# A graph layer in split single precision: one stationary operand for the edge sums, the bias moved to ScalarE

## What is computed

```python
h = jnp.maximum(_layernorm(x, axis=-1), 0.0)
agg = jax.ops.segment_sum(edge_features, tgt, num_segments=N_NODES)
counts = jax.ops.segment_sum(jnp.ones(...), tgt, num_segments=N_NODES)
agg = agg / jnp.maximum(counts, 1.0)[:, None]
combined = jnp.concatenate([agg, h], axis=1)
out = x + jax.nn.relu(combined @ W1 + b1) @ W2 + b2
```

## Time and profile before

| | |
|---|---|
| runs, median of 3 | 1381.35 us (1381.05 to 1381.44) |
| the profiled execution, its own time | 1381.12 us |
| its span, first to last instruction | 1379.1 us |
| mean granted TensorE clock | 0.989 of full speed |
| busy: PE / PEld | 1340.5 us / 1122.1 us |
| busy: DVE / ACT / POOL | 1202.3 us / 696.5 us / 533.0 us |

### The profile page before, as it was taken

One profiled execution on the slowest core, in us unless ns is written; L12 is line 12 of the kernel. 1 busy time (PEld: TensorE's weight loads), 2 busy tenths in 40 slices (PEclk: granted clock), 3 DMA queues, 4 the chain that ended last, 5 costly groups with the idle time before them and its releaser, 6 DMA issues.

```text
span 1379.1 us, 29845 instructions
## 1 busy us (share of the span) xinstructions
PE 1340.5 (97%) x7078; PEld 1122.1 (81%) x7078; DVE 1202.3 (87%) x2979; ACT 696.5 (51%) x1280; POOL 533.0 (39%) x709
## 2 busy tenths in 40 slices
PE   2799999999999999999999999999999999999998
PEld 0588888888888888888888888888888888888887
DVE  7598989898888989898988888898889898898986
ACT  3354545455554545454555545454545555454543
POOL 4334343433333343434333343434343443434341
PEclk7899999999999999999999999999999999999999
DMA  5567676766767676867667676758676766767672
GB/s 108 89 122 136 115 143 110 138 113 135 116 132 129 119 138 113 143 111 138 114 135 115 133 131 117 133 118 142 109 141 113 136 117 131 120 129 132 118 128 56
DMA packets 424904, 169.49 MB, mean 123 GB/s; under 512 B 323190, under 2 KB 424506, under 8 KB 424892
## 3 DMA queue, kind: packets, MB, share of 16 engines
q1 hardware_dynamic: 421608, 167.40, 67.0%
q10 hardware_dynamic: 3284, 1.97, 0.8%
HBM read 66.50 MB, written 51.40 MB: 85 GB/s over the span
## 4 chain that ended last, share of the span: by engine, by line
PE 96%; DVE 2%; DMA 1%; SPq 1%; issue 0%
PE P L815 26%; PE P L817 14%; PE P L795 13%; PE P L797 13%; PE P L796 13%; PE P L804 7%; PE P L805 7%; PE PA L785 2%; PE PA L784 2%; DVE below L597 1%; DMA X<-in_x_dram 0%; DMA dst_a<-in_dst_dram 0%; SPq L275 0%; DMA table_dram<-table 0%; SPq L276 0%
## 5 line engine op out<-in xcount | busy, mean ns | idle before, releaser
L815 PE MATMUL P<-w_both,H_hi 128*128 128x512 f32 x1568 | 552.1, 393 | 4.7 <-DVE H_lo L646 4.7
L530 ACT ACTIVATE H_hi<-P 128x512 fp32r<-128x512 f32 x392 | 234.6, 599 | 509.9 <-PE P L805 509.9
L817 PE MATMUL P<-w_both,H_lo 128*128 128x256 f32 x1568 | 442.5, 282 | 0.0
L646 DVE SCALAR_TENSOR_TENSOR H_lo<-P,H_hi 128x512 fp32r<-128x512 f32 x392 | 268.8, 686 | 108.4 <-ACT H_hi L530 101.8
L815 PEld LDWEIGHTS P<-w_both,H_hi 128*128 128x128 f32 x1568 | 295.3, 188 | 71.0 <-DVE H_lo L646 6.2
L795 PE MATMUL P<-HT_hi,w_hi 128*128 128x512 f32 x784 | 316.0, 403 | 19.5 <-DVE HT_lo L638 19.5
L797 PE MATMUL P<-HT_hi,w_lo 128*128 128x512 f32 x784 | 310.8, 396 | 0.0
L796 PE MATMUL P<-HT_lo,w_hi 128*128 128x512 f32 x784 | 310.4, 396 | 0.0
L817 PEld LDWEIGHTS P<-w_both,H_lo 128*128 128x128 f32 x1568 | 297.0, 189 | 4.5
L409 POOL TENSOR_TENSOR XB<-X,b_row 128x1024 f32<-128x1024 f32 x98 | 234.9, 2397 | 137.9 <-DVE O L657 137.9
L403 POOL TENSOR_TENSOR E_lo<-ES,E_hi 128x256 fp32r<-128x256 f32 x98 | 73.1, 746 | 416.0 <-ACT E_hi L510 416.0
(11 more groups left out here) (72 smaller groups left out, 1136.9 us busy)
## 6 DMA issues: line engine op xcount, KB each, us to landing
X<-in_x_dram SPq DMA_DIRECT2D x98, 512.0 KB, 4.2
HQ<-HN SPq DMA_DIRECT2D x388, 128.0 KB, 4.2
out_dram<-O SPq DMA_DIRECT2D x97, 512.0 KB, 4.8
ER<-in_edge_attr_dram SPq DMA_DIRECT2D x392, 32.0 KB, 1.8
DT<-table_dram SPq DMA_DIRECT2D x392, 1.0 KB, 1.7
w_raw<-in_L_gnn_W_dram ACTq DMA_DIRECT2D x4, 128.0 KB, 7.2
w_raw<-in_L_gnn_W_dram ACTq DMA_DIRECT2D x2, 256.0 KB, 8.6
HQ<-HN ACTq DMA_DIRECT2D x4, 128.0 KB, 4.1
```

Of the source, the lines that this page charges most:

```text
L530: act.activation(H1_hi[:, m, :], bank(m)[:], ACT.Relu).then_inc(s_1hi, 1)
L646: dve.scalar_tensor_tensor(out=H1_lo[:, m, :], in0=bank(m)[:], scalar=0.0, in1=H1_hi[:, m, :], op0=ALU.max, op1=ALU.subtract).then_inc(s_1 ...
L815: pe.matmul(out_bank(j)[:], H1_hi[:, m, rows], w2_both[:, m, :, :].rearrange("p a d -> p (a d)"), start=(m == 0), stop=False)
L817: last = pe.matmul(out_bank(j)[:, 0:D], H1_lo[:, m, rows], w2_both[:, m, 0, :], start=False, stop=(m == CH - 1))
```

## The change

It has three parts.

- E_hi and E_lo become two halves of one tile, E_both, so that a group's edges form one stationary operand of 128 columns. `edge_means` issues 4 products instead of 8; PA now has 128 rows, the sums of the high parts in rows 0 to 63 and those of the low parts in rows 64 to 127.
- QA is now the rounding of all 128 rows of PA, against W1's edge rows twice (wa_hi). QB holds the rounded sums in rows 0 to 63, against the low part of those weights, and in rows 64 to 127, in place of the ones, what rounding the high sums left over, against the high part.
- b1 is no longer a row of wb_lo. It is loaded as a column (b1_col), and ACT adds it as it applies the relu. ACT now reads each PSUM bank twice: once for H_hi, once for H1, the same relu in full precision; DVE subtracts the two from SBUF.

```diff
-            pool.memset(b1_raw[:], 0.0).then_inc(s_zero, 1)
...
-            pool.memset(QB[DE:P, :].bitcast(F32), 1.0).then_inc(s_const, 1)
...
-                pool.tensor_tensor(E_lo[b][:], ES[b][:], E_hi[b][:], ALU.subtract).then_inc(s_elo, 1)
+                pool.tensor_tensor(E_both[b][:, :, 1, :], ES[b][:], E_both[b][:, :, 0, :], ALU.subtract).then_inc(s_elo, 1)
...
-            for p in (64, 96):
-                act.dma_start(b1_raw[p:p + 1, :], b1.rearrange("(o h) -> o h", o=1)).then_inc(s_w[2], 16)
+            act.dma_start(b1_col[:], b1.rearrange("(m p) -> p m", p=P),
+                          allow_slow_non_contiguous=True).then_inc(s_w[2], 16)
...
-                act.activation(QB[0:DE, :], PA[0:DE, :], ACT.Copy).then_inc(s_qhi, 1)
+                act.activation(QA[:], PA[:], ACT.Copy).then_inc(s_qhi, 1)
                 act.wait_ge(s_qhi, 2 * t + 1)
-                act.activation(QA[0:DE, :], QB[0:DE, :], ACT.Copy).then_inc(s_qhi, 1)
+                act.activation(QB[0:DE, :], QA[0:DE, :], ACT.Copy).then_inc(s_qhi, 1)
...
-                    act.activation(H1_hi[:, m, :], bank(m)[:], ACT.Relu).then_inc(s_1hi, 1)
+                    act.activation(H1_hi[:, m, :], bank(m)[:], ACT.Relu, bias=b1_col[:, m:m + 1]).then_inc(s_1hi, 1)
+                    act.activation(H1[:, m, :], bank(m)[:], ACT.Relu, bias=b1_col[:, m:m + 1]).then_inc(s_1, 1)
...
-            act.activation(b1_hi[DE:P, :], b1_raw[DE:P, :], ACT.Copy).then_inc(s_whi, 1)
-            act.activation(wb_lo[64:96, :], b1_raw[64:96, :], ACT.Copy).then_inc(s_whi, 1)
+            act.activation(wb_lo[DE:P, :], wa_raw[DE:P, :], ACT.Copy).then_inc(s_whi, 1)
...
-                dve.tensor_tensor(QA[DE:P, :], PA[0:DE, :], QB[0:DE, :], ALU.subtract).then_inc(s_qlo, 1)
+                dve.tensor_tensor(QB[DE:P, :], PA[0:DE, :], QA[0:DE, :], ALU.subtract).then_inc(s_qlo, 1)
...
-                dve.scalar_tensor_tensor(out=H1_lo[:, m, :], in0=bank(m)[:], scalar=0.0, in1=H1_hi[:, m, :],
-                                         op0=ALU.max, op1=ALU.subtract).then_inc(s_1lo, 1)
+                dve.wait_ge(s_1, CH * t + m + 1)
+                dve.tensor_tensor(H1_lo[:, m, :], H1[:, m, :], H1_hi[:, m, :], ALU.subtract).then_inc(s_1lo, 1)
...
-            dve.tensor_tensor(wb_lo[96:P, :], b1_raw[96:P, :], b1_hi[96:P, :], ALU.subtract).then_inc(s_wblo, 1)
...
-                    pe.matmul(PA[0:DE, cols], E_hi[b][:, k, :], OH[b][:, k, :], start=(k == 0), stop=False)
-                    last = pe.matmul(PA[0:DE, cols], E_lo[b][:, k, :], OH[b][:, k, :], start=False, stop=(k == SUB - 1))
+                    last = pe.matmul(PA[:, cols], E_both[b][:, k, :, :].rearrange("p a d -> p (a d)"), OH[b][:, k, :],
+                                     start=(k == 0), stop=(k == SUB - 1))
```

More of the change, by code:

```diff
@@ L89, in build @@
         wa_raw = sb("wa_raw", [P, H])
-        b1_raw = sb("b1_raw", [P, H])
+        b1_col = sb("b1_col", [P, CH])
         w2_raw = sb("w2_raw", [P, CH, D])
@@ L95, in build @@
         wb_lo = sb("wb_lo", [P, H], F32R)
-        b1_hi = sb("b1_hi", [P, H], F32R)
         w2_both = sb("w2_both", [P, CH, 2, D], F32R)
@@ L138, in build @@
         ES = [sb(f"ES{b}", [P, SUB, DE]) for b in range(2)]
-        E_hi = [sb(f"E_hi{b}", [P, SUB, DE], F32R) for b in range(2)]
-        E_lo = [sb(f"E_lo{b}", [P, SUB, DE], F32R) for b in range(2)]
+        E_both = [sb(f"E_both{b}", [P, SUB, 2, DE], F32R) for b in range(2)]
         OH = [sb(f"OH{b}", [P, SUB, P], F32R) for b in range(2)]
@@ L146, in build @@
         QB = sb("QB", [P, TILE], F32R)
+        H1 = sb("H1", [P, CH, TILE])
         H1_hi = sb("H1_hi", [P, CH, TILE], F32R)
@@ L226, in build @@
         s_1hi = sem("s_1hi")
+        s_1 = sem("s_1")
         s_1lo = sem("s_1lo")
@@ L353, in _ @@
             pool.memset(dst_b[:], 1 << 20).then_inc(s_zero, 1)
-            pool.memset(b1_raw[:], 0.0).then_inc(s_zero, 1)
             pool.iota(thresholds[:], pattern=[[P, KS], [TILE, TILES]], base=0, channel_multiplier=0,
                       allow_small_or_imprecise_dtypes=True).then_inc(s_zero, 1)
-            pool.wait_ge(s_zero, 3)
+            pool.wait_ge(s_zero, 2)
             pool.iota(thresholds[:, :, TILES - 1:TILES], pattern=[[P, KS], [0, 1]], base=LAST, channel_multiplier=0,
@@ L375, in _ @@
             pool.wait_ge(s_const, 10)
-            pool.memset(QB[DE:P, :].bitcast(F32), 1.0).then_inc(s_const, 1)
+            pool.memset(ident[:], 0.0).then_inc(s_const, 1)
             pool.wait_ge(s_const, 11)
-            pool.memset(ident[:], 0.0).then_inc(s_const, 1)
-            pool.wait_ge(s_const, 12)
             pool.affine_select(out=ident[:], in_=ident[:], compare_op=ALU.not_equal, fill=1.0, base=0,
@@ L415, in _ @@
             pool.tensor_tensor(w1_lo[:], w1_raw[:], w1_hi[:], ALU.subtract).then_inc(s_wlo, 1)
-            pool.wait_ge(s_whi, 5)
+            pool.wait_ge(s_whi, 4)
             pool.tensor_tensor(w2_both[:, :, 1, :], w2_raw[:], w2_both[:, :, 0, :], ALU.subtract).then_inc(s_wlo, 1)
@@ L491, in _ @@
                 act.dma_start(wa_raw[a * DE:(a + 1) * DE, :], w1[0:DE, :]).then_inc(s_w[1], 16)
-            act.wait_ge(s_zero, 3)
-            for p in (64, 96):
-                act.dma_start(b1_raw[p:p + 1, :], b1.rearrange("(o h) -> o h", o=1)).then_inc(s_w[2], 16)
+            act.dma_start(b1_col[:], b1.rearrange("(m p) -> p m", p=P),
+                          allow_slow_non_contiguous=True).then_inc(s_w[2], 16)
             for a in range(2):
@@ L509, in edges_high @@
                 past(act, s_sum, t - 1)
-                act.activation(E_hi[b][:], ES[b][:], ACT.Copy).then_inc(s_ehi, 1)
+                act.activation(E_both[b][:, :, 0, :], ES[b][:], ACT.Copy).then_inc(s_ehi, 1)
             def transposed_high(t):
@@ L535, in _ @@
             act.activation(wa_hi[:], wa_raw[:], ACT.Copy).then_inc(s_whi, 1)
-            act.wait_ge(s_w[2], 32)
-            act.activation(b1_hi[DE:P, :], b1_raw[DE:P, :], ACT.Copy).then_inc(s_whi, 1)
-            act.activation(wb_lo[64:96, :], b1_raw[64:96, :], ACT.Copy).then_inc(s_whi, 1)
+            act.activation(wb_lo[DE:P, :], wa_raw[DE:P, :], ACT.Copy).then_inc(s_whi, 1)
+            act.wait_ge(s_w[2], 16)
             act.wait_ge(s_w[3], 32)
@@ L749, in _ @@
             onehot(0, 0)
-            dve.wait_ge(s_whi, 3)
+            dve.wait_ge(s_whi, 2)
             dve.tensor_tensor(wb_lo[0:DE, :], wa_raw[0:DE, :], wa_hi[0:DE, :], ALU.subtract).then_inc(s_wblo, 1)
-            dve.tensor_tensor(wb_lo[96:P, :], b1_raw[96:P, :], b1_hi[96:P, :], ALU.subtract).then_inc(s_wblo, 1)
             means_low(0)
@@ L774, in _ @@
             pe.matmul(PA[0:1, 0:1], ones_f[0:EP, :], fall[:], start=True, stop=True).then_inc(s_found, 1)
-            pe.wait_ge(s_const, 13)
+            pe.wait_ge(s_const, 12)
             def edge_means(t, b):
@@ L846, in _ @@
             pe.wait_ge(s_wlo, 2)
-            pe.wait_ge(s_wblo, 2)
-            pe.wait_ge(s_whi, 5)
+            pe.wait_ge(s_wblo, 1)
+            pe.wait_ge(s_whi, 4)
             step(0, 0)
```

## The result

| | before | changed |
|---|---|---|
| median of the runs | 1381.39 us (1381.05 to 1384.72) | 1448.19 us (1447.89 to 1448.84) |
| ratio | | 1.0482, 95% interval 1.0467 to 1.0496 |
| the profiled execution, its own time | 1381.12 us | 1447.89 us |
| its span; mean granted TensorE clock | 1379.1 us; 0.989 | 1446.3 us; 0.989 |

What follows compares the result with a forecast made beforehand. PE was taken to bound the kernel, at 13.54 us a tile. Stop less edge gain, 96 x (0.23 - 0.09) = 13.4 us, on 1381.1 gave 1394.5 us, 1.0% slower; range 1376 to 1412, the forecast's own 1388 to 1401.

Steps and rivals of the forecast that it cites:

- H_lo itself keeps its length: DVE's hidden-layer subtraction: 686 ns before with one operand in PSUM, 687 ns for L638 wholly from SBUF, so no lengthening.
- PE's stop: Ahead of the first product with block 3, PE waits for a late H_lo: 0.23 us a tile, bounds 0.05 and 0.41.
- the start of block 2's H_lo: On DVE, H_lo of block 2 also waits for the second activation and starts 0.64 us later, at 719.00.
- the edge sums: Edge stage on PE, four products on 128 columns instead of eight: PE gains 0.53 - 0.44 = 0.09 us a tile.
- the bias operand: ACT's two activations read the bias from a tile: 0.09 us more on the interval and on the length.
- the means: Second products of the means cost PE nothing; DVE's part arrives just in time, with 0.06 us remaining.
- b1's load: At the start, b1 fetched in 512 four-byte pieces: 6.8 us, covered by ACT's 9.89 us wait for POOL.
- The signs: Wrong if the PE-from-H_lo line has few entries, the waits show the means instead, or the tile is under 13.54 us.
- the line that the forecast named: "PE P <- DVE H_lo" in the waits of PE, with some 96 entries and about 20 us.
- The fifth: Rival: the means come late too, for instance through each H_lo's second wait; 0.10 us there gives 1404 us; chance 0.09.
- The first: Rival: all 0.18 us falls on ACT's bias operand, stop 0.41, tile loses 0.32, 1412 us; chance 0.12.
- The second: Rival: second activation fits into DVE's slack at block 2's H_lo (0.41 us); 1377 or 1372.5 us; chance 0.09.

Runs made afterwards that it cites:

- last version: Changed kernel with one biased activation, H_lo as max(sum, -b1) - H_hi from PSUM, missing b1 put back through b2: 1373.67 us, ratio 0.9943.
- the third experiment: Changed kernel without DVE's wait for the first activation (s_1hi), H_lo still with both operands in SBUF: 1407.09 us, ratio 1.0184.

## Why the prediction was wrong, point by point

The 66.8 us, put together from the medians of the runs (those of the kernel before differ by up to 0.2 us):

| step | from, to | us |
|---|---|---|
| merged edge sums, one activation with bias, low part from PSUM | before 1381.2, last version 1373.7 | -7.5 |
| second activation, plain, and two waits; no bias operand | 1373.7, 1389.45 | +15.8 |
| bias operand on both activations | 1389.45, 1406.4 | +16.9 |
| both operands of H_lo in SBUF | 1406.4, 1448.2 | +41.8 |

The last step has no price of its own: it is 41.8 us with both waits, 6.6 with one, and 23 in the kernel before, as the start of H_lo falls against XB's.

- **The step that failed: "H_lo itself keeps its length: 686 ns before with one operand in PSUM, and 687 ns for L638".** The rows are right and the inference isn't. The prediction put the lengthening at nothing; H_lo took 1066 ns in the mean, 1719 beside an XB and 679 elsewhere, and with both waits in place that is 41.8 of the 66.8 us. L638 is the same operation, but not beside the same neighbour, as the timeline of the kernel before shows:

```profile
701.10 0.69 DVE L646 SCALAR_TENSOR_TENSOR H_lo<-P,H_hi 128x512 fp32r<-128x512 f32 x1
701.20 2.40 POOL L409 TENSOR_TENSOR XB<-X,b_row 128x1024 f32<-128x1024 f32 x1 [1.44 <-DVE O L657]
...
702.44 0.69 DVE L646 SCALAR_TENSOR_TENSOR H_lo<-P,H_hi 128x512 fp32r<-128x512 f32 x1
...
707.78 0.62 POOL L398 TENSOR_TENSOR ES<-ER,DT 128x256 f32<-128x256 f32 x1
708.29 0.67 DVE L638 TENSOR_TENSOR HT_lo<-HT,HT_hi 128x512 fp32r<-128x512 f32 x1
```

  L638 meets POOL for 0.11 us at most here, with the tail of a short ES (over the trace 65 of 196 do, for 0.16 us at most). H_lo lies inside the 2.4 us of XB (702.44), untouched only because it had one operand in PSUM. The prediction priced the operation alone and did not ask what runs on POOL at the time. The Trainium skill has the rule (SBUF — State Buffer, sections SBUF: two separate sides and Who interferes with whom): a DVE instruction with two SBUF inputs contends with a GpSimd instruction that reads SBUF, one with at most one SBUF input does not (outside the 2-port modes), and the second to start is blocked until the first is done. This case's traces agree on each of the three: 2.85 against 0.68 us, 0.69 with one operand in PSUM, and the reversal in the third experiment.
- **Mis-sized: PE's stop, 0.23 us a tile.** Without the exclusion (operand in PSUM) the tile takes 13.81 us, and with the 0.08 us saved on the edges added back the stop is 0.35. (In the rows block 3's product is 0.23 us late here too, but the forecast's 0.23 held its load, and the rows have that behind the start, as in the odd tile above.) The chain missed in one place, the start of block 2's H_lo: forecast 1.26 us after H_hi's start, measured 1.37 (723.28 to 724.65). The second activation ends 1.27 us after that start (1.24 forecast), and H_lo follows 0.10 us later, where the prediction took 0.02 from a row with one wait. With one wait, 5.9 us return. From there on the chain ran as forecast: 1.89 us from that H_lo to block 3's, against 1.90, and 0.05 us from its end to PE.
- **Right: the edge sums.** Four products take 0.40 us from their first to L790 (706.09, 706.49), and L791 follows at 706.77: 0.68 us against 0.76. That is 0.08 of the 0.09 us forecast. The whole tile gains 0.08 in the last version. The estimate from the Trainium skill's 81 ns (TensorE: Matmul & The Clock Gate, Back-to-back issue gap) was too hopeful here: by the trace's records the second product starts 0.06 us after the first, the others and L790 0.11 us apart.
- **Right: the bias operand** (0.09 us, twice), the means, and b1's load. PE waits for the means 1.6 us in the whole run. At the start the first product of layer 1 stands at 33.98 us against 33.80.
- **The signs could not warn.** The waits of PE show the line that the forecast named:

```profile
PE P L810 <- DVE H_lo L643: 35.2, 98, 2.4
```

  Its 98 entries are the 96 expected, with 35.2 us for about 20, and PE is busy 95% of the span. The signs of being wrong did not cover H_lo's own length.
- **The rivals.** None had the exclusion. The fifth came nearest in kind, the second wait of each H_lo, but placed its cost at the means. The first named ACT's operand for a time of 1412 us; it costs what the forecast said. The second was right that H_lo of block 2 decides with 0.41 us to spare, which is why the last version is free, and wrong that the second activation fits in.

## What to carry to other kernels

Before an elementwise operand moves from PSUM to SBUF, list what GpSimd does at that time: a row for the same operation elsewhere is a price only if its neighbours are the same. When a group's mean rises and no work was added, split it by what lies beside it in the timeline. And a remedy can be sought on either engine: leave one operand in PSUM, cut the other engine's long instruction into pieces, or let the short one go first.

## What the runs showed of the hardware

- A DVE subtraction of 128x512 with both operands in SBUF and a POOL addition of 128x1024 exclude each other for a whole instruction: the held H_lo ends 0.55 us after the addition in 97 cases, whatever its start. With one operand in PSUM the same pair runs together at 0.69 and 2.40 us.
- Which of them stands still was settled by about 0.1 us of start time, so one wait more or less on DVE moved the run by 41 us, where the same wait was worth 5.9 us without the exclusion.
- Two waits ahead of a DVE instruction instead of one made it start some 0.07 us later after the same release (0.10 against 0.03 us, medians over the tiles). Which part of the sequencer takes them is not settled by these runs.
- Two plain activations that read the same PSUM bank follow each other after 0.49 us. The one pair of different banks behind the earlier trace rows starts 0.48 us apart (45.83 and 46.31, from the single starts); the prediction's 0.46 took off the mean length of 0.60 where the first of the pair has 0.58. That is about half of the 0.03 us by which the interval was under-sized; the cause of the rest was not tried.
